# Attention kernel: the low rotary key products on 64 rows of TensorE, two score pieces at a time, with the rotary halves laid out by head

## The chip, the cores and the metric

The kernel runs on one core of one Trainium2 chip. The metric is the device time of one execution in microseconds; the median of three runs of the kernel before is 1512.42 us (1511.95 to 1512.44).

## What is computed

One layer over 2048 tokens of width 512: a layer norm, causal attention with a latent of 128 for keys and values and 16 heads, each head's key being 128 plain numbers and 64 rotary ones shared by all heads, and beside it a sum of eight 512x512 factors.

```python
q = (x @ wq).reshape(b, s, H, QH).transpose(0, 2, 1, 3)
q_nope, q_pe = (q[..., :NOPE], q[..., NOPE:])
kva = x @ wkv_a
ckv, k_pe = (kva[..., :LORA], kva[..., LORA:])
ckv = ckv * jax.lax.rsqrt(jnp.mean(ckv * ckv, axis=-1, keepdims=True) + EPS)
ckv = ckv * kv_norm_scale
kv = (ckv @ wkv_b).reshape(b, s, H, NOPE + VD).transpose(0, 2, 1, 3)
...
q_pe = _rope(q_pe, cos, sin)
k_pe = _rope(k_pe[:, None, :, :], cos, sin)
...
scores = jnp.einsum('bhqd,bhkd->bhqk', qs, ks_) * scale
...
attn = jax.nn.softmax(scores, axis=-1)
out = jnp.einsum('bhqk,bhkd->bhqd', attn, v)
```

## The kernel before

The weights of keys are absorbed into those of the queries, so that scores are products of a query's latent (128) and the common latent keys, plus a rotary part of 64. All operands are kept as two fp16 parts, a high one and a low one (the rest), and a product of two such numbers takes three products of TensorE: high with high, high with low, low with high.

Queries are taken in four chunks of 512, the last chunk first (`ORDER` is 3, 2, 1, 0). Within a chunk the 16 heads follow one another; a head of a chunk is a unit `i` (64 in all). A unit has four rows `r` of 128 queries, and a row of chunk `c` has `c + 1` score pieces `p` of up to 512 keys: 512 each and last `(r + 1) * 128`; for `r == 0` the last two are 384 and 256. So the first 16 units have four pieces in a row, the next 16 three, then two, then one.

A score piece is the function `scores`, with its products on lines 547, 548 and 549 (latent: `kTh` and `kTl` are the high and low keys, `q[:, i % 2, 0]` and `[1]` the high and low queries), 552 and 553 (rotary). The rotary query tile `q[:, i % 2, 2]` has 128 rows: the 64 high parts of the head and its 64 low parts. `kRh` and `kRl`, the rotary keys, stand twice in their 128 rows, so that L552 gives high and low queries with the high keys in one product, and L553 both with the low keys. Pieces go round four banks of PSUM (`s_bank`, `SBANKS = 4`): piece n waits for the exponentials of piece n - 4 (semaphore `a_exp`). L553 of a piece tells VectorE that it is done (`p_s`).

After the pieces of a row TensorE has other work in a fixed order written out by `fills(i, r)`: the next query products ("q", "pe"), value products of the unit before (`values`), output products (`head_output`), weights to be prepared in the first 16 units. `three` (lines 400 to 402) issues the three products of each of these.

Each row then goes: VectorE takes each piece's maximum (`maxima`: L1134 for whole pieces, L1136 with the causal mask for the last), the row's (L1146), and the bias `nm` (L1153); ScalarE takes the exponentials (`exps`, L781, with the sums) and their high parts (`high_parts`, L791); GpSimd takes the low parts (`low_parts`, L1354); SyncE's queue transposes both by DMA (L1539) for the value products of the next unit. On ScalarE, in rows 0 and 1 of the units with three or four pieces, the work that comes early (`early`: query read-out L764, output weights L748, rotary query L770) stands right behind the exponentials of piece 2 and the high part of piece 1, and ahead of the exponentials of piece 3 where there is one.

The rotary queries are made for two heads at once: `q_rope` on TensorE, then on VectorE L1121 to L1123 (cosine products of 128 rows, sine products of 2 times 64 rows, reading the other half), the sum on GpSimd (L1330), and for each head the copy of the high part on ScalarE (`rope_parts`, L770, all 128 rows of both heads) and on GpSimd two subtractions of 32 rows (L1345), which put the head's low parts over the other head's rows. The four blocks of 32 rows are ordered half first, head second. `load_wp` brings the rotary columns of the weights in four loads; `turned_keys` and `latent` make the rotary keys, in the opening.

Of the kernel before, what the change touches and what calls it, by code (L numbers as in the profile page):

```python
# [8 lines left out]
ALU = mybir.AluOpType  # L9
# [3 lines left out]
P = 128  # L13
# [3 lines left out]
CH = 512  # L17
# [33 lines left out]
def chunk(i):  # L51

    return ORDER[i // H]
# [12 lines left out]
def pieces(c, r):  # L66

    w = [CH] * c + [(r + 1) * P]
    if c and r == 0:
        w[c - 1:] = [CH - P, 2 * P]  # L70
    return [(sum(w[:p]), n) for p, n in enumerate(w)]
# [143 lines left out]
def build(nc, x, wq, wkv_a, wkv_b, wo, kvs, factors, bias, rope_t, rope_n, out):  # L215
    ctx = ExitStack()
    with ctx:
        def sb(name, shape, dt):
            return ctx.enter_context(nc.sbuf_tensor(name, shape, dt))
# [57 lines left out]
        rstd = sb("rstd", [P, 3, NT], F32)  # L277
        ssq = sb("ssq", [P, 3, NT], F32)
        ps = ctx.enter_context(nc.psum_tensor("ps", [P, 8, CH], F32))
        q = sb("q", [P, 2, 3, CH], F16)  # L280


        with ExitStack() as stage_one:
# [114 lines left out]
        def _(e):  # L398
# [132 lines left out]
            def scores(i, r, p):  # L531
                n = piece(i, r, p)
                k0, keys = pieces(chunk(i), r)[p]
                b = s_bank(n)[:, 0:keys]
                qs, ks = slice(r * P, (r + 1) * P), slice(k0, k0 + keys)
                if n >= SBANKS:
                    e.wait_ge(z["a_exp"], n - SBANKS + 1)
                if n < SBANKS:

                    e.wait_ge(z["v_kva"], NP - SBANKS + 1 + n)  # L540
                    e.wait_ge(z["a_kk"], NP - SBANKS + 1 + n)
                if i == 0 and r == 0 and p < NC - 1:

                    e.wait_ge(z["v_kT"], (p + 2) * QT // 2)
                if r == 0 and p == 0:
                    e.wait_ge(z["v_q"], i + 1)
                e.matmul(b, q[:, i % 2, 0, qs], kTh[:, ks], start=True, stop=False)  # L547
                e.matmul(b, q[:, i % 2, 0, qs], kTl[:, ks], start=False, stop=False)  # L548
                e.matmul(b, q[:, i % 2, 1, qs], kTh[:, ks], start=False, stop=False)  # L549
                if r == 0 and p == 0:  # L550
                    e.wait_ge(z["g_parts"], 2 * i + 2)
                e.matmul(b, q[:, i % 2, 2, qs], kRh[:, ks], start=False, stop=False)  # L552
                e.matmul(b, q[:, i % 2, 2, qs], kRl[:, ks], start=False, stop=True).then_inc(z["p_s"], 1)  # L553

            def values(i, part):

# [93 lines left out]
        def _(e):  # L650
# [53 lines left out]
            def squares(kind, i):  # L704

                w, at, total, load, loads = {
                    "sqp": (wsp[:, :, :].rearrange("p k n -> p (k n)"), 0, nrm[:, 2:3], "d_wp", 64),
                    "sq0": (wsq[:, 0, :, :].rearrange("p k n -> p (k n)"), E, nrm[:, 0:1], "d_wq0", 16),
                    "sq1": (wsq[:, 1, :, :].rearrange("p k n -> p (k n)"), 2 * E, nrm[:, 1:2], "d_wq1", 16),
                    "sqk": (wsk[:, i % 4:i % 4 + 2, :].rearrange("p a n -> p (a n)"), 3 * E, rows[:, 0:1], "g_sk", 1)}[kind]  # L710
                e.wait_ge(z[load], loads * (i // 2 + 1))
                if i:
                    e.wait_ge(z["p_nrm"], i // 2)
                    e.wait_ge(z["a_" + kind], i // 2)
                if i and kind == "sqk":
                    e.wait_ge(z["a_r4"], i // 2)
                square_sum(w, at, total).then_inc(z["a_" + kind], 1)
                if kind == "sqk":

                    e.wait_ge(z["a_sqk"], i // 2 + 1)  # L720
                    if i:
                        e.wait_ge(z["a_r8"], i // 2)
                    e.activation(rows[:, 1:2], rows[:, 0:1], ACT.Square).then_inc(z["a_r4"], 1)
                    e.wait_ge(z["a_r4"], i // 2 + 1)
                    e.activation(nrm[:, 3:4], rows[:, 1:2], ACT.Square).then_inc(z["a_r8"], 1)
# [40 lines left out]
            def rope_parts(i):  # L766
                e.wait_ge(z["g_rot"], i // 2 + 1)
                if i >= 2:
                    e.wait_ge(z["p_s"], FIRST[i - 1])
                e.activation(q[:, i % 2, 2, :], rot[:, 0, :], ACT.Copy).then_inc(z["a_parts"], 1)  # L770

            def exps(i, r, p):
# [124 lines left out]
        def _(e):  # L897
# [177 lines left out]
            def latent(p2):  # L1075
                b = latent_bank(p2)
                ts = slice(2 * p2, 2 * p2 + 2)
                rows = both(p2)
                cos = ropen[:, rows, 0, :].unsqueeze(2).broadcast_to([P, 2, 2, HALF])
                halves = b[:, :, LORA:QH].rearrange("p t (a n) -> p t a n", a=2)  # L1080
                turned = kt[p2 % 4][:, :, P:2 * P].rearrange("p t (a d n) -> p t a d n", a=2, d=2)
                if p2 == 0:
                    e.wait_ge(z["d_ropen"], 16)
                e.wait_ge(z["a_rms"], p2 + 1)
                e.reciprocal(ssq[:, 2, ts], ssq[:, 1, ts]).then_inc(z["v_rr"], 1)
                if p2 >= 4:
                    e.wait_ge(z["p_kT"], p2 - 3)
                e.tensor_tensor(turned[:, :, :, 0, :], halves, cos, ALU.mult)
                for a in range(2):

                    ins = e.tensor_tensor(ktmp[:, p2 % 4, :, a, :], halves[:, :, 1 - a, :], ropen[:, rows, 1 + a, :], ALU.mult)
                ins.then_inc(z["v_kva"], 1)
# [21 lines left out]
            def q_rope(i):  # L1114
                b = bank(("pe", i))
                if i % H == 0:
                    e.wait_ge(z["d_tab"], 16 * (i // H + 1))
                e.wait_ge(z["p_pe"], i // 2 + 1)
                if i:
                    e.wait_ge(z["g_parts"], 2 * i)  # L1120
                e.tensor_tensor(rot[:, 0, :], b, tab[:, 0, :], ALU.mult)  # L1121
                e.tensor_tensor(rot[0:ROPE, 1, :], b[ROPE:P, :], tab[0:ROPE, 1, :], ALU.mult)
                e.tensor_tensor(rot[ROPE:P, 1, :], b[0:ROPE, :], tab[ROPE:P, 1, :], ALU.mult).then_inc(z["v_pe"], 1)  # L1123

            def maxima(i, r, p):
                n = piece(i, r, p)
# [147 lines left out]
        def _(e):  # L1274
# [17 lines left out]

            def turned_keys(p2):

                turned = kt[p2 % 4][:, :, P:2 * P].rearrange("p t (a d n) -> p t a d n", a=2, d=2)
                e.wait_ge(z["v_kva"], p2 + 1)
                for d in (1, 0):
                    ins = e.tensor_tensor(turned[:, :, :, d, :], turned[:, :, :, 0, :], ktmp[:, p2 % 4, :, :, :],
                                          ALU.add)
                ins.then_inc(z["g_kk"], 1)  # L1300
# [31 lines left out]
            def rope_parts(i):  # L1332

                e.wait_ge(z["a_parts"], i + 1)
                if i == 0:
                    e.wait_ge(z["g_rot"], 1)
                    e.wait_ge(z["g_kk"], NP - 1)
                else:
                    r = 2 if i % H == 0 else 1 if i < (NC - 1) * H else 0
                    e.wait_ge(z["g_pL"], piece(i - 1, r, chunk(i - 1)) + 1)  # L1340
                hi = q[:, i % 2, 2, :]
                for half in range(2):
                    src = slice((2 * half + i % 2) * HALF, (2 * half + i % 2 + 1) * HALF)
                    dst = slice((2 * half + 1 - i % 2) * HALF, (2 * half + 2 - i % 2) * HALF)
                    e.tensor_tensor(hi[dst, :], rot[src, 0, :], hi[src, :], ALU.subtract).then_inc(  # L1345
                        z["g_parts"], 1)
                    e.wait_ge(z["g_parts"], 2 * i + half + 1)
# [59 lines left out]
        def _(e):  # L1407
# [39 lines left out]
            def load_wp(i):  # L1447
                if i:
                    e.wait_ge(z["v_wpe"], i // 2)

                for half in range(2):
                    for b in range(2):
                        at, src = (2 * half + b) * HALF, (i + b) * QH + NOPE + half * HALF
                        e.dma_start(wsp[:, :, at:at + HALF], wqv[:, :, src:src + HALF]).then_inc(z["d_wp"], 16)

            def load_factor(i):
                r, k4 = divmod(i, KE)
# [173 lines left out]
def rope_tables():  # L1631

    inv = (1.0 / np.float32(10000.0) ** (np.arange(0, ROPE, 2, dtype=np.float32) / np.float32(ROPE)))
    ang = (np.arange(S, dtype=np.float32)[:, None] * inv.astype(np.float32)).astype(np.float32)
    cos, sin = np.cos(ang), np.sin(ang)
    by_row = np.empty((P, 2, S), np.float32)
    cos, sin = cos * np.float32(BACK), sin * np.float32(BACK)
    by_row[:, 0] = np.tile(cos.T, (4, 1))
    by_row[:, 1] = np.concatenate([-sin.T, -sin.T, sin.T, sin.T])
    by_pos = np.stack([cos, -sin, sin], 1).reshape(NT, P, 3, HALF).transpose(1, 0, 2, 3)  # L1640
    return by_row, np.ascontiguousarray(by_pos)

# [18 lines left out]
```

## Time and profile before

| | |
|---|---|
| median of three runs | 1512.42 us |
| the profiled execution, its own time | 1514.25 us |
| its span, first to last instruction | 1512.4 us |
| TensorE (PE) busy | 1474.0 us, 97% |
| VectorE (DVE) busy | 1012.4 us, 67% |
| ScalarE (ACT) busy | 969.0 us, 64% |
| GpSimd (POOL) busy | 906.8 us, 60% |
| DMA queue q1, share of 16 engines' span | 73.6% |

Busy times overlap, so they don't add up. The four chunks can be told by the first products of L547 in units 0, 16 and 32, at 56.3, 604.4 and 1012.4 us; ahead of 56 us lies the opening, in which keys and values are made. Ends of TensorE's products in a trace are modelled, so its pace is read from starts.

### The profile page before, as it was taken

To read this page: it belongs to the slowest core of one execution; us is meant where nothing else is said; L and a number is where in the kernel's file an instruction comes from. 1 tells how busy PE (TensorE), PEld (TensorE's weight loads), DVE (VectorE), ACT (ScalarE), POOL (GpSimd) and SP (SyncE) were. 2 spreads that over 40 slices of the span, in tenths; PEclk is the share of its full clock that TensorE was granted. 3 is DMA by queue.
4 is the path that set the end of the run, shared out by engine and by line. 5 is a ranking of instruction groups with operands and counts; after the bars stand their busy time and mean duration, and the time that the engine had idled before them with its cause. 6 is when DMAs were issued, how large, how long until landed. Compare 5 with 4: busy or idle time off the path is not lost.

```text
span 1512.4 us, 25752 instructions
## 1 busy us (share of the span) xinstructions
PE 1474.0 (97%) x7908; PEld 757.4 (50%) x7908; DVE 1012.4 (67%) x2563; ACT 969.0 (64%) x2410; POOL 906.8 (60%) x913
## 2 busy tenths in 40 slices
PE   5899999999999999999999999999999999999997
PEld 5544555554454544545444444445555555455553
DVE  7767676777777766655556565566656666676776
ACT  7877777677766576666466666665556566554553
POOL 1688777766665465675465656656546555664552
PEclk9999999999999999999999999999999999999999
DMA  6499989897776598787577677877856777754554
GB/s 200 144 197 207 191 184 187 190 176 147 152 153 137 120 185 170 133 176 139 119 147 140 138 133 146 179 146 139 150 117 135 142 133 151 159 133 94 121 117 100
DMA packets 646615, 227.84 MB, mean 151 GB/s; under 512 B 599376, under 2 KB 612176, under 8 KB 646096
## 3 DMA queue, kind: packets, MB, share of 16 engines
q1 hardware_dynamic: 646480, 226.20, 73.6%
q8 instruction: 65, 1.06, 0.3%
q14 instruction: 70, 0.57, 0.1%
HBM read 65.67 MB, written 17.83 MB: 55 GB/s over the span
## 4 chain that ended last, share of the span: by engine, by line
PE 83%; DVE 6%; ACT 6%; issue 3%; DMA 1%; POOL 0%; ACTq 0%; SPq 0%; POOLq 0%; DVEq 0%
PE ps L400 17%; PE ps L401 17%; PE ps L402 16%; PE ps L547 7%; PE ps L552 6%; PE ps L553 6%; PE ps L549 6%; PE ps L548 6%; ACT ex L781 4%; DVE gm L1134 2%; DVE ps L1136 1%; DVE q L1111 0%; ACT wV L748 0%; DMA acc<-x_in 0%; DVE nm L1153 0%
## 5 line engine op out<-in xcount | busy, mean ns | idle before, releaser
L1354 POOL TENSOR_TENSOR st<-ex,st 128x512 f16<-128x512 f32 (+3 forms) x640 | 637.1, 1014 | 504.0 <-ACT st L791 493.8
L781 ACT ACTIVATE ex<-ps,nm,scales 128x512 f32<-128x512 f32 (+3 forms) x640 | 452.0, 709 | 466.8 <-DVE nm L1153 456.3
L1134 DVE TENSOR_REDUCE gm<-ps 128x1 f32<-128x512 f32 (+1 forms) x384 | 248.7, 668 | 168.6 <-PE ps L553 164.5
L791 ACT ACTIVATE st<-ex 128x512 f16<-128x512 f32 (+3 forms) x640 | 341.5, 562 | 5.9
L547 PE MATMUL ps<-kTh,q 128*128 128x512 f16 (+3 forms) x640 | 222.3, 347 | 8.0 <-ACT ex L781 5.7
L400 PE MATMUL ps<-pT,vH 128*128 128x512 f16 (+3 forms) x640 | 222.3, 347 | 2.3 <-DMA pT<-st 2.3
L552 PE MATMUL ps<-kRh,q 128*128 128x512 f16 (+3 forms) x640 | 222.2, 347 | 1.4 <-POOL q L1345 1.4
L401 PE MATMUL ps<-pT,vH 128*128 128x512 f16 (+3 forms) x640 | 222.4, 347 | 0.0
L549 PE MATMUL ps<-kTh,q 128*128 128x512 f16 (+3 forms) x640 | 222.2, 347 | 0.0
L553 PE MATMUL ps<-kRl,q 128*128 128x512 f16 (+3 forms) x640 | 222.2, 347 | 0.0
L548 PE MATMUL ps<-kTl,q 128*128 128x512 f16 (+3 forms) x640 | 222.2, 347 | 0.0
L402 PE MATMUL ps<-pT,vL 128*128 128x512 f16 (+3 forms) x640 | 219.2, 348 | 0.0
L1187 DVE SCALAR_TENSOR_TENSOR acc<-ps,rden,acc 128x512 f32<-128x512 f32 x256 | 189.7, 743 | 4.4 <-PE ps L402 4.0
L1345 POOL TENSOR_TENSOR q<-rot,q 32x512 f16<-32x512 f32 x128 | 148.8, 1162 | 25.6 <-ACT q L770 12.8
L1136 DVE CUSTOM_DVE_ANT_0 ps<-ps,cmask 128x256 f32<-128x256 f32 (+3 forms) x256 | 132.7, 518 | 25.6 <-PE ps L553 22.8
L781 ACT ACTIVATION_READ_ACCUMULATOR ex<-ps,nm,scales 128x1 f32 x640 | 125.7, 196 | 0.0
L1111 DVE SCALAR_TENSOR_TENSOR q<-ps,q 128x512 f16<-128x512 f32 x64 | 44.2, 690 | 112.5 <-ACT q L764 112.4
L400 PE MATMUL ps<-wV,oT 128*128 128x512 f16 x256 | 98.0, 383 | 4.7 <-issue 3.1
L547 PEld LDWEIGHTS ps<-kTh,q 128*128 128x128 f16 x640 | 62.5, 98 | 75.3 <-ACT ex L781 11.2
L401 PE MATMUL ps<-wV,oT 128*128 128x512 f16 x256 | 98.0, 383 | 0.0
L402 PE MATMUL ps<-wV,oT 128*128 128x512 f16 x256 | 97.8, 382 | 0.0
L400 PE MATMUL ps<-xT,wA 128*128 128x512 f16 x256 | 97.1, 379 | 0.0
(200 smaller groups left out, 2144.7 us busy)
## 6 DMA issues: line engine op xcount, KB each, us to landing
wA<-w_abs SPq DMA_DIRECT2D x48, 256.0 KB, 2.9
wV<-w_vo SPq DMA_DIRECT2D x48, 256.0 KB, 2.9
pT<-st SPq DMA_TRANSPOSE x640, 3.3
fland<-factors_in SPq DMA_DIRECT2D x28, 256.0 KB, 3.1
wP<-w_pe SPq DMA_DIRECT2D x24, 256.0 KB, 3.1
wsq<-wq_in SPq DMA_DIRECT2D x16, 256.0 KB, 3.8
wso<-wo_in SPq DMA_DIRECT2D x16, 256.0 KB, 3.1
w_abs<-wA SPq DMA_DIRECT2D x16, 256.0 KB, 2.3
```

The lines of the kernel that those rows point to most:

```text
L400: e.matmul(o, a[0], b[0], start=first, stop=False)
L401: e.matmul(o, a[0], b[1], start=False, stop=False)
L402: return e.matmul(o, a[1], b[0], start=False, stop=last)
L547: e.matmul(b, q[:, i % 2, 0, qs], kTh[:, ks], start=True, stop=False)
L548: e.matmul(b, q[:, i % 2, 0, qs], kTl[:, ks], start=False, stop=False)
L549: e.matmul(b, q[:, i % 2, 1, qs], kTh[:, ks], start=False, stop=False)
L552: e.matmul(b, q[:, i % 2, 2, qs], kRh[:, ks], start=False, stop=False)
L553: e.matmul(b, q[:, i % 2, 2, qs], kRl[:, ks], start=False, stop=True).then_inc(z["p_s"], 1)
L781: e.activation(ex[:, n % NEX, 0:keys], s_bank(n)[:, 0:keys], ACT.Exp, bias=nm[:, (i * QT + r) % 4:(i * QT + r) % 4 + 1], scale=scales[:, p ...
L791: e.activation(stage(n, keys)[:, :, 0, :], ex[:, n % NEX, 0:keys].rearrange("p (t n) -> p t n", n=P), ACT.Copy).then_inc(z["a_pH"], 1)
L1134: e.tensor_reduce(m, b, AX_X, ALU.max).then_inc(z["v_max"], 1)
L1354: e.tensor_tensor(s[:, :, 1, :], ex[:, n % NEX, 0:keys].rearrange("p (t n) -> p t n", n=P), s[:, :, 0, :], ALU.subtract).then_inc(z["g_pL" ...
```

## The change

1. `q` gets a fourth slot, `q[:, :, 3]`, which holds the 64 high rotary parts of the head twice, in rows 0 to 63 and 64 to 127. `rope_parts` on ScalarE writes it with two copies of 64 rows, ahead of the copy that was there.
2. L553 is replaced. For an odd piece p two products follow its L552: pieces p - 1 and p each with 64 rows (the low keys' first copy for the one, the second for the other), each telling of its own piece. The product of low queries and low keys, which was part of L553, is left out for them. The low product of an even piece is thereby issued behind the four first products of the piece after it. A last piece with an even number (chunks 2 and 0) keeps L553 with 128 rows.
3. The four blocks of 32 rows are ordered head first, half second, in the weights (`load_wp`: two loads of 64 columns for four of 32), the sine table, the keys (`turned`) and GpSimd's subtractions. VectorE's sine products become four of 32 rows.

```diff
@@ q
-        q = sb("q", [P, 2, 3, CH], F16)
+        q = sb("q", [P, 2, 4, CH], F16)
@@ scores
-                e.matmul(b, q[:, i % 2, 2, qs], kRl[:, ks], start=False, stop=True).then_inc(z["p_s"], 1)
+                if p % 2 == 0 and p == chunk(i):
+
+                    e.matmul(b, q[:, i % 2, 2, qs], kRl[:, ks], start=False, stop=True).then_inc(z["p_s"], 1)
+                elif p % 2:
+
+                    for half in range(2):
+                        k0, keys = pieces(chunk(i), r)[p - 1 + half]
+                        on, ks = slice(half * ROPE, (half + 1) * ROPE), slice(k0, k0 + keys)
+                        e.matmul(s_bank(n - 1 + half)[:, 0:keys], q[on, i % 2, 3, qs], kRl[on, ks], start=False,
+                                 stop=True).then_inc(z["p_s"], 1)
@@ squares (scalar)
-                    "sqp": (wsp[:, :, :].rearrange("p k n -> p (k n)"), 0, nrm[:, 2:3], "d_wp", 64),
+                    "sqp": (wsp[:, :, :].rearrange("p k n -> p (k n)"), 0, nrm[:, 2:3], "d_wp", 32),
@@ rope_parts (scalar)
+
+                mine = slice(i % 2 * ROPE, (i % 2 + 1) * ROPE)
+                for half in range(2):
+                    e.activation(q[half * ROPE:(half + 1) * ROPE, i % 2, 3, :], rot[mine, 0, :], ACT.Copy)
                 e.activation(q[:, i % 2, 2, :], rot[:, 0, :], ACT.Copy).then_inc(z["a_parts"], 1)
@@ latent (vector) and turned_keys (gpsimd)
-                turned = kt[p2 % 4][:, :, P:2 * P].rearrange("p t (a d n) -> p t a d n", a=2, d=2)
+                turned = kt[p2 % 4][:, :, P:2 * P].rearrange("p t (d a n) -> p t a d n", a=2, d=2)
@@ q_rope (vector)
-                e.tensor_tensor(rot[0:ROPE, 1, :], b[ROPE:P, :], tab[0:ROPE, 1, :], ALU.mult)
-                e.tensor_tensor(rot[ROPE:P, 1, :], b[0:ROPE, :], tab[ROPE:P, 1, :], ALU.mult).then_inc(z["v_pe"], 1)
+                for n in range(4):
+
+                    to, of = slice(n * HALF, (n + 1) * HALF), slice((n ^ 1) * HALF, ((n ^ 1) + 1) * HALF)
+                    ins = e.tensor_tensor(rot[to, 1, :], b[of, :], tab[to, 1, :], ALU.mult)
+                ins.then_inc(z["v_pe"], 1)
@@ rope_parts (gpsimd)
-                    src = slice((2 * half + i % 2) * HALF, (2 * half + i % 2 + 1) * HALF)
-                    dst = slice((2 * half + 1 - i % 2) * HALF, (2 * half + 2 - i % 2) * HALF)
+                    src = slice((2 * (i % 2) + half) * HALF, (2 * (i % 2) + half + 1) * HALF)
+                    dst = slice((2 - 2 * (i % 2) + half) * HALF, (3 - 2 * (i % 2) + half) * HALF)
@@ load_wp (sync)
-                for half in range(2):
-                    for b in range(2):
-                        at, src = (2 * half + b) * HALF, (i + b) * QH + NOPE + half * HALF
-                        e.dma_start(wsp[:, :, at:at + HALF], wqv[:, :, src:src + HALF]).then_inc(z["d_wp"], 16)
+                for b in range(2):
+                    src = (i + b) * QH + NOPE
+                    e.dma_start(wsp[:, :, b * ROPE:(b + 1) * ROPE], wqv[:, :, src:src + ROPE]).then_inc(z["d_wp"], 16)
@@ rope_tables
-    by_row[:, 1] = np.concatenate([-sin.T, -sin.T, sin.T, sin.T])
+    by_row[:, 1] = np.concatenate([-sin.T, sin.T, -sin.T, sin.T])
```

## Rows read from the trace of the kernel before

**Rows 1.** The page: busy us of the engines, and the chain that ended last.

```profile
PE 1474.0 (97%) x7908; PEld 757.4 (50%) x7908; DVE 1012.4 (67%) x2563; ACT 969.0 (64%) x2410; POOL 906.8 (60%) x913
...
PE 83%; DVE 6%; ACT 6%; issue 3%; DMA 1%; POOL 0%; ACTq 0%; SPq 0%; POOLq 0%; DVEq 0%
```

**Rows 2.** TensorE in order of time, unit 8, row 0: start us, us, what.

```profile
323.81 0.38 PE L547 MATMUL ps<-kTh,q 128*128 128x512 f16 x1
...
325.97 0.33 PE L547 MATMUL ps<-kTh,q 128*128 128x384 f16 x1
...
326.78 0.27 PE L547 MATMUL ps<-kTh,q 128*128 128x256 f16 x1
...
327.22 0.27 PE L553 MATMUL ps<-kRl,q 128*128 128x256 f16 x1
```

**Rows 3.** Stretches: length, busy us of each engine, granted clock, DMA share, GB/s.

```profile
56.50:609.00 552.50, 542.92 (x2895) 275.33 (x2894) 397.55 (x1000) 393.54 (x991) 371.49 (x359) 1.00 0.83 167
609.00:1000.00 391.00, 391.00 (x1995) 193.22 (x1994) 230.99 (x545) 244.68 (x597) 234.22 (x226) 1.00 0.75 146
...
1300.00:1512.00 212.00, 200.86 (x1115) 103.67 (x1113) 151.92 (x395) 108.25 (x259) 108.14 (x114) 0.98 0.53 115
```

**Rows 4.** TensorE's groups by shape: busy us, mean ns, idle before.

```profile
L553 PE MATMUL ps<-kRl,q 128*128 128x512 f16 x400 | 151.6, 379 | 0.0
...
L553 PE MATMUL ps<-kRl,q 128*128 128x384 f16 x112 | 36.5, 326 | 0.0
...
L553 PE MATMUL ps<-kRl,q 128*128 128x256 f16 x112 | 30.5, 273 | 0.0
```

**Rows 5.** In order of time, unit 8: fp32 transposes between fp16 products.

```profile
335.36 0.60 PE L424 MATMUL ps<-ident,wsq 128*128 128x128 f32 x4
...
335.79 0.27 PE L431 MATMUL ps<-ident,wsk 128*128 128x128 f32 x1
...
336.01 0.38 PE L400 MATMUL ps<-pT,vH 128*128 128x512 f16 x1
```

**Rows 6.** Weight loads in order of time, behind a wait, unit 8.

```profile
342.91 0.10 PEld L547 LDWEIGHTS ps<-kTh,q 128*128 128x128 f16 x1 [0.76 <-ACT ex L781]
```

**Rows 7.** In order of time, unit 7, rows 1 and 2: ScalarE and TensorE.

```profile
308.36 0.62 ACT L770 ACTIVATE q<-rot 128x512 f16<-128x512 f32 x1
...
308.88 0.56 ACT L781 ACTIVATE ex<-ps,nm,scales 128x256 f32<-128x256 f32 x1
...
309.32 0.20 ACT L781 ACTIVATION_READ_ACCUMULATOR ex<-ps,nm,scales 128x1 f32 x1
...
309.91 0.33 PE L547 MATMUL ps<-kTh,q 128*128 128x384 f16 x1
```

**Rows 8.** VectorE in order of time, unit 8, row 0.

```profile
326.17 1.37 DVE L1134 TENSOR_REDUCE gm<-ps 128x1 f32<-128x512 f32 x2 [0.39 <-PE ps L553]
327.53 0.43 DVE L1136 CUSTOM_DVE_ANT_0 ps<-ps,cmask 128x256 f32<-128x256 f32 x1
327.88 0.14 DVE L1136 DVE_READ_ACCUMULATOR2_ANT gm<- 128x1 f32 x1
```

**Rows 9.** In order of time, unit 8, rows 1 and 2.

```profile
342.66 0.20 ACT L781 ACTIVATION_READ_ACCUMULATOR ex<-ps,nm,scales 128x1 f32 x1
...
342.92 0.34 PE L547 MATMUL ps<-kTh,q 128*128 128x384 f16 x1 [0.26 <-ACT ex L781]
```

**Rows 10.** TensorE's waits, 56 to 609 us: us in total, times, longest.

```profile
PE ps L547 <- ACT ex L781: 5.7, 10, 1.4
```

**Rows 11.** ScalarE in order of time, at the turn to unit 8.

```profile
325.72 0.20 ACT L781 ACTIVATION_READ_ACCUMULATOR ex<-ps,nm,scales 128x1 f32 x1
```

**Rows 12.** The chain that ended last, opening: start us, us, what.

```profile
44.07 0.69 DVE rot L1121
...
45.48 0.68 DVE rot L1123
...
47.00 0.33 PE ps L493
```

More of the change, by code:

```diff
@@ L1293, in turned_keys @@
             def turned_keys(p2):
-                turned = kt[p2 % 4][:, :, P:2 * P].rearrange("p t (a d n) -> p t a d n", a=2, d=2)
+                turned = kt[p2 % 4][:, :, P:2 * P].rearrange("p t (d a n) -> p t a d n", a=2, d=2)
                 e.wait_ge(z["v_kva"], p2 + 1)
```

## The prediction

> **What bounds the kernel now.** I read the page's busy shares and its chain of waits first: TensorE is busy 1474.0 us of 1512.4 and holds 83% of the chain that ended last [rows 1]. A busy TensorE need not be a full one, so I read the pace next, in the list of instructions in order of time. Ten score products of 512 columns start between 323.81 and 325.97 us, 0.216 us each; five of 384 columns take 0.81 us (0.162 each) and four of 256 take 0.44 (0.11 each) [rows 2]. That is a stream without holes at 2.4 GHz, so a column saved is time saved wherever TensorE does not then wait. The table of stretches shows where it does not wait today: from 609 to 1000 us (three pieces) it is busy 391.00 of 391.00 us, in the first chunk (56.5 to 609 us) 542.92 of 552.50, at the granted clock of 1.00 [rows 3]. The other engines are busy 60 to 67% on average, but each row of scores has a loop through them: last score of a row, its maximum on VectorE, the bias, four exponentials on ScalarE, and only then a free bank for the next row's last piece. How much play that loop has decides the change.
>
> **The products that go.** The fifth product of a score piece (L553) streams 512, 384 or 256 columns or 128 [rows 4]. A pair (pieces 0 and 1, and 2 and 3) now runs its two fifth products on different halves of the rows; if they run together, a pair costs the longer one. Columns saved by a unit (one head of one chunk) are the shorter of each pair, over its four rows: with four pieces 512+256, 512+256, 512+384 and 512+512, so 3456; with three 384+512+512+512 = 1920; with two 256+256+384+512 = 1408; with one none. Times 16 heads and 0.216 us for 512: 23.3 + 13.0 + 9.5 = 45.8 us, in 128 + 64 + 64 = 256 pairs. This saving has two preconditions that no row of before shows, since all products there use 128 rows: that the halves run side by side, and that going from 128 rows to 64 and back is cheap.
>
> **What a pair costs besides.** From below: nothing, and not less, since no work disappears other than the columns counted. From above: TensorE lets the last product leave the array before each of the two changes of form. A 512-column product has a record of 379 ns at a pace of 216, so 0.163 us lie behind the stream (its end is modelled), 0.33 us a pair [rows 2, 4]. The nearest rows on changing the way of working are the fp32 transposes between fp16 products: 335.36 to 335.79, then 336.01, each at its stream's time, no gap [rows 5]. An exposed weight load is seen after a wait: load at 342.91, product at 342.92 [rows 6]. I take 0.015 us a pair, nearest to these rows: 240 pairs, 3.6 us (of 256, some 16 lie ahead of a wait that swallows it). The Trainium skill, "TensorEngine Tiling (Array Packing)", Key Properties, says that changing the tiling mode, other than the tile, drains TensorE; the first rival below is what that would do here. Its page "TensorE: Matmul & The Clock Gate", Part 3, says of row tiles that products on distinct row groups start some 4 ns apart, which would give the 45.8 us; no run shows either yet.
>
> **What ScalarE and VectorE get, and what is late next.** Two copies of 64 rows go ahead of the copy at L770, in row 1 of a unit, before its last exponential. A copy takes ScalarE 0.52 us (308.36 to 308.88) [rows 7]; half the rows hold as many elements each, so I price two at 1.04 us. Queued behind them are the exponential of piece 3, the high parts and through them GpSimd; waiting for that exponential is TensorE's piece 3 of row 2. Count the play of this boundary in the first chunk, where four pieces use all four banks. (a) TensorE comes sooner after its own last score of row 1: pair 0/1 is 0.216 us shorter and piece 2's low product moves behind piece 3, another 0.216: 0.43. (b) Piece 2 and 3 are released together, so piece 2's maximum (half of 1.37 us, 0.68) no longer lies under piece 3's products (0.54 us for 256 columns); VectorE already runs close behind, 326.17 to 327.53 for the 512s and on to 327.88 [rows 8]. That is 0.54 us later, 0.68 for wider last pieces. (c) 1.04 us of copies. Together 2.0 us. The play today: in unit 7 the reading of the exponential's sum ends at 309.52 and TensorE starts at 309.91, 0.39 us [rows 7]; a stall of 1.6 us is due. In unit 8 TensorE waits already, 0.26 us, until the same reading ends at 342.86 and its product starts at 342.92 [rows 9]; there VectorE's scale work is what is late, (b) is only the 0.33 us by which TensorE's row ends sooner, and the stall grows by 1.8. Today such waits make 5.7 us in ten [rows 10], which stay. I take 7 and 8 for odd and even units and 13 of 16 units, since unit 0 and two late ones have more play or take the copies elsewhere: 13 x 1.75 = 22.8 us. At the turn from row 3 to the next unit's row 0 the play is 326.78 - 325.92 = 0.86 us [rows 2, 11] against 0.38 (piece 2 has 384 columns) + 0.68: 0.2 us in 14 units, 2.8. The turns from row 0 and row 2 I leave at nothing: their play hides it, and without that cover each would cost up to 0.5 us a unit, 8 us. So the first chunk gives back 25.6 us and earns nothing of its 23.3.
> With three pieces or two, a row does not use all four banks and the copies come behind the last exponential; I cost them at nothing, covered by TensorE's fills, and the 22.5 us stay. With one piece nothing is gained and ScalarE gets 1.04 us a unit in a stretch where TensorE is busy 200.86 of 212 [rows 3]: 0 to 3 us, taken as 0.
>
> **Small edits.** The rotary sums take four operations of 32 rows where two of 64 stood; each is as long as its 512 columns, 0.69 us, so 1.38 us a pair of heads on VectorE, and GpSimd's sum behind it. In the loop they stand where VectorE waits for scores anyway. In the opening they don't: rot starts at 44.07, the third ends at 46.16, the key parts follow, and a transpose of TensorE waits for these until 47.00 [rows 12]. That is 1.4 us on the path. The opening's copies end before the query product does. The two loads of 64 rotary columns for four of 32 take two issues off SyncE's queue for each pair of heads and move the same bytes, nothing gained as nobody on the path waits for them; the orders of halves in keys, queries and sine table change places, not counts; GpSimd's two operations per head stay.
>
> **The sum.** -45.8 + 25.6 + 3.6 + 1.4 = -15.2 us on the profiled execution's 1514.25, which stands 1.8 above the median of 1512.42: 1499.1 there, 1497 as a median.
>
> **Rivals.** 1. Slower: TensorE empties at every change of form. For it: the 0.163 us behind each stream must go somewhere if the array may not hold both forms. Against it: [rows 5]. It decides from (45.8 - 25.6 - 1.4)/240 = 0.078 us a pair. With those terms alone the sum is -18.8. At half the bound, 0.163 a pair, 39.1 us come on top: +20.3, 1533; at the full bound 78.2 us, +59.4, 1572. 2. The change doesn't do what it says: the halves run one after the other. Then no column is saved, the deferral (0.216), the later maximum (some 0.4 odd, 0 even) and the copies still cost row 2 some 1.28 us in 13 units, 16.6, and the opening 1.4: 1530. 3. The loop has more play than I count, and 15 of the 25.6 us of stalls don't come: 1482. 4. A change of form costs about 0.08 us a pair: all is eaten, 1512.
>
> **How the numbers follow.** Forecast 0.42 (its own range 1487 to 1508), rival 1 0.27, rival 2 0.15, rival 3 0.08, rival 4 0.08. Some 0.2% (3 us) is about what a measurement of this kernel can tell from no change. Faster: forecast and rival 3 less an edge, 0.48. Same: rival 4 and the edge, 0.09. Slower: 0.43. The range reaches from rival 3 to a drain of three quarters of its bound (58.7 - 18.8 = 39.9), 1482 to 1552; outside lie some 0.05 below and 0.12 above.
>
> **What would show it.** Side by side: L553's successors of a pair start within 0.05 us of each other; serial: 0.2 us apart. Drain: gaps of 0.04 us and more ahead of the 64-row products and behind them, in the stretch behind 609 us too. Stalls: TensorE waiting for the exponential some 25 us more, nearly all before 609 us, ahead of piece 3 of row 2; the first chunk as long as before and the stretches with three and two pieces 13.0 and 9.5 us shorter. I am wrong if the first chunk shrinks by over 10 us, if copies of 64 rows take other than 0.5 us, or if the opening does not grow by a microsecond.

## The result and the profile after

The changed kernel takes 1559.62 us (median of four runs, 1555.75 to 1562.61) against 1512.29 us for the kernel before: 1.0312 of its time, 95% interval 1.0285 to 1.0339, 47 us slower. The forecast was 1497 us, and the time lies above its range of 1482 to 1552.

The page of the changed kernel, the lines that answer to [rows 1], and two groups of its fifth part (busy us, mean ns, idle time before them and what ended it):

```profile
PE 1491.4 (96%) x7908; PEld 710.2 (46%) x7908; DVE 1045.7 (67%) x2627; ACT 1049.6 (67%) x2538; POOL 906.7 (58%) x913
...
PE 75%; ACT 9%; DVE 9%; issue 4%; DMA 1%; POOL 0%; ACTq 0%; SPq 0%; POOLq 0%; DVEq 0%
...
L547 PE MATMUL ps<-kTh,q 128*128 128x512 f16 (+3 forms) x640 | 224.1, 350 | 30.0 <-ACT ex L794 27.5
...
L561 PE MATMUL ps<-kRl,q 64*128 64x512 f16 (+2 forms) x512 | 98.4, 367 | 0.0
```

TensorE's share of the chain fell from 83% to 75%, and ScalarE and VectorE have 9% each instead of 6. The low products (L561, and L555 for the pieces without a partner, 39.2 us) are busy 137.6 us together where L553 was busy 222.2, so columns did go. But the chain has waits that were not there, and TensorE's records, which overlap, hide something else, which only the list in order of time shows. From 609 us on, in the stretch of three pieces:

```profile
700.79 0.38 PE L552 MATMUL ps<-kRh,q 128*128 128x512 f16 x1
701.11 0.39 PE L561 MATMUL ps<-kRl,q 64*128 64x512 f16 x2
701.43 0.28 PE L547 MATMUL ps<-kTh,q 128*128 128x256 f16 x1
```

and the weight loads in the same place:

```profile
701.10 0.10 PEld L561 LDWEIGHTS ps<-kRl,q 64*128 64x128 f16 x2 [0.42 <-issue]
...
701.42 0.10 PEld L547 LDWEIGHTS ps<-kTh,q 128*128 128x128 f16 x1 [0.23 <-issue]
```

Two products stand in one row of 0.39 us, as long as one: they run side by side, the second starting 3 or 4 ns behind the first in 254 of the 256 pairs. The Trainium skill, "TensorE: Matmul & The Clock Gate", Part 3, says about 4 ns for row tiles, and the trace agrees. But L552 starts at 700.79 and at a pace of 0.216 us the pair was due at 701.01; it starts at 701.11. It streams to 701.33, and the next product starts at 701.43. Both times TensorE stands still for 0.10 us. The weight load, which elsewhere is issued under the running product, comes only at the end of the gap, 0.01 us ahead of its product, as close as behind a plain wait [rows 6]. So load and product are held back together, and the gap is not the time of the load.

Where the time went, by stretch: the opening, and then the chunks with four, three, two and one pieces in a row, told by the first product of L547 in units 0, 16, 32 and 48 of each trace (us; the next section describes the kernels of the other rows):

| kernel | opening | four | three | two | one |
|---|---|---|---|---|---|
| before | 56.3 | 548.1 | 408.0 | 297.1 | 202.9 |
| changed | 58.4 | 581.7 | 409.8 | 302.9 | 207.1 |
| e1_layout | 57.8 | 550.2 | 408.1 | 299.6 | 207.7 |
| e10_four_ops | 57.3 | 548.5 | 408.1 | 299.6 | 207.9 |
| e2_copies | 58.9 | 564.1 | 408.1 | 299.6 | 208.8 |
| e3_defer | 57.6 | 554.2 | 409.2 | 299.6 | 209.0 |
| e4_pairs128 | 57.4 | 576.1 | 409.2 | 300.4 | 208.3 |
| e5_same_rows | 58.5 | 592.1 | 421.6 | 311.6 | 206.4 |
| e6_single64 | 57.5 | 596.2 | 448.2 | 323.4 | 217.6 |
| e7_copies_late | 58.3 | 553.3 | 409.8 | 302.9 | 207.2 |
| e11_pairs128_late | 58.3 | 552.2 | 409.2 | 299.7 | 210.0 |
| e9_batch | 58.5 | 614.6 | 410.5 | 303.6 | 207.0 |
| e9b_batch_late | 58.8 | 577.9 | 410.5 | 303.4 | 206.9 |
| e8_before_late | 56.1 | 545.0 | 408.0 | 297.1 | 203.0 |

No stretch got shorter. The four pieces have 33.6 of the 47.5 us.

In these 33.6 us lies a term that no list of waits shows. TensorE's granted clock fell to half four times among the four pieces of the changed kernel, for 17.1 us in all, 16.3 of them busy; in the kernel before it was once, for 3.4 us. Two of the four (columns as in [rows 3]):

```profile
89.20:92.61 3.41, 3.41 (x10) 1.22 (x8) 0.99 (x2) 3.16 (x10) 2.84 (x4) 0.50 1.03 195
...
147.23:154.06 6.83, 6.09 (x16) 2.04 (x17) 3.76 (x8) 4.51 (x12) 5.25 (x5) 0.50 0.51 101
```

At half the clock half of the busy time is lost: an estimate of 8.2 us against 1.7, 6.5 us more. How often the clock falls differs from trace to trace (not at all in this stretch of e10_four_ops, 10.2 us in e4_pairs128), so differences of a few us in the column of four pieces need a look at it.

### The profile page after: what moved, and what is told of

The parts are those of the page before. It is cut to its first block, busy times and chain, and to the rows that moved or that the text cites. A ratio compares the mean times of both kernels' runs of the same rounds, so it can differ in the third digit from the quotient of the medians.

```text
span 1560.0 us, 25928 instructions
## 1 busy us (share of the span) xinstructions
PE 1491.4 (96%) x7908; PEld 710.2 (46%) x7908; DVE 1045.7 (67%) x2627; ACT 1049.6 (67%) x2538; POOL 906.7 (58%) x913
## 4 chain that ended last, share of the span: by engine, by line
PE 75%; ACT 9%; DVE 9%; issue 4%; DMA 1%; POOL 0%; ACTq 0%; SPq 0%; POOLq 0%; DVEq 0%
PE ps L400 16%; PE ps L402 15%; PE ps L401 15%; PE ps L547 7%; PE ps L552 6%; PE ps L549 6%; PE ps L548 6%; ACT ex L794 5%; PE ps L561 4%; DVE gm L1150 2%; PE ps L555 1%; ACT q L782 1%; DVE ps L1152 1%; ACT wV L757 1%; DVE rot L1138 1%
## 5 line engine op out<-in xcount | busy, mean ns | idle before, releaser
L1150 DVE TENSOR_REDUCE gm<-ps 128x1 f32<-128x512 f32 (+1 forms) x384 | 244.8, 668 | 215.3 <-PE ps L561 214.4
L547 PE MATMUL ps<-kTh,q 128*128 128x512 f16 (+3 forms) x640 | 224.1, 350 | 30.0 <-ACT ex L794 27.5
L552 PE MATMUL ps<-kRh,q 128*128 128x512 f16 (+3 forms) x640 | 222.6, 348 | 3.0 <-POOL q L1361 3.0
L547 PEld LDWEIGHTS ps<-kTh,q 128*128 128x128 f16 x640 | 62.2, 97 | 116.5 <-ACT ex L794 43.2
L561 PE MATMUL ps<-kRl,q 64*128 64x512 f16 (+2 forms) x512 | 98.4, 367 | 0.0
```

The costliest lines, as they stand in the source:

```text
L1150: e.tensor_reduce(m, b, AX_X, ALU.max).then_inc(z["v_max"], 1)
```

## The experiments

Two theories stood against each other. One: the change of rows (from products of 128 rows to products of 64 and back) eats what the columns give. The other: the loop of maxima, exponentials and banks carries the loss. The first kernels put the parts of the change in one by one.

**The layout alone.** The low product is as before, the copies are out; what is left is the order of halves and VectorE's four operations.

```diff
@@ scores
...
-                elif p % 2:
...
-                    for half in range(2):
...
+                e.matmul(b, q[:, i % 2, 2, qs], kRl[:, ks], start=False, stop=True).then_inc(z["p_s"], 1)
@@ rope_parts (scalar)
-                mine = slice(i % 2 * ROPE, (i % 2 + 1) * ROPE)
-                for half in range(2):
-                    e.activation(q[half * ROPE:(half + 1) * ROPE, i % 2, 3, :], rot[mine, 0, :], ACT.Copy)
```

> The changed kernel with the low product of each piece put back as it was (128 rows, right behind the piece's other four) and without the two copies of 64 rows: the change of layout alone, with VectorE's four sine products of 32 rows. Both theories, that of the change of rows (TensorE pays some 0.1 us at each change between 128 and 64 rows) and that of the loop (waits for the exponentials carry the loss), put the layout at little: 1514 to 1519 us, about 2 us of it in the opening, nothing in the stretches of three and two pieces.

Measured: 1524.85 us, 1.0076 of before (1.0061 to 1.0091). Both theories were too low here; the table puts 4.8 us into the stretch of one piece and 2.5 into that of two. In the stretch of one piece, VectorE and TensorE in order of time in the layout kernel:

```profile
1389.18 2.79 DVE L1126 TENSOR_TENSOR rot<-ps,tab 32x512 f32<-32x512 f32 x4
...
1392.64 0.68 DVE L1176 SCALAR_TENSOR_TENSOR oT<-ps,oT 128x512 f16<-128x512 f32 x1
...
1393.42 0.38 PE L400 MATMUL ps<-wV,oT 128*128 128x512 f16 x1 [0.48 <-issue]
```

and VectorE at the same point of a later pair of heads in the kernel before, with TensorE's product:

```profile
1466.04 0.68 DVE L1123 TENSOR_TENSOR rot<-ps,tab 64x512 f32<-64x512 f32 x1
...
1467.39 0.68 DVE L1172 SCALAR_TENSOR_TENSOR oT<-ps,oT 128x512 f16<-128x512 f32 x1
...
1468.93 0.38 PE L400 MATMUL ps<-wV,oT 128*128 128x512 f16 x1
```

The rotary operations are followed on VectorE by the row's maximum, the bias and the low part of the values' output (`oT`), for which TensorE's output product waits. Before, that part ended at 1468.07, 0.86 us ahead of the product. VectorE's 1.38 us more are 0.5 too many, and TensorE stands 0.64 us behind its pace in five of the stretch's eight pairs of heads and 1.20 in a sixth, 4.4 us (in the stretch of two pieces 0.42 in six of eight, 2.5 us). The trace names "issue" as what ended the wait, since the releasing engine had just been done.

**VectorE's operations alone, in the kernel before.**

```diff
-                e.tensor_tensor(rot[0:ROPE, 1, :], b[ROPE:P, :], tab[0:ROPE, 1, :], ALU.mult)
-                e.tensor_tensor(rot[ROPE:P, 1, :], b[0:ROPE, :], tab[ROPE:P, 1, :], ALU.mult).then_inc(z["v_pe"], 1)
+                for n in range(4):
+                    to, of = slice(n * HALF, (n + 1) * HALF), slice((n ^ 2) * HALF, ((n ^ 2) + 1) * HALF)
+                    ins = e.tensor_tensor(rot[to, 1, :], b[of, :], tab[to, 1, :], ALU.mult)
+                ins.then_inc(z["v_pe"], 1)
```

> The kernel before with VectorE's two sine products of 64 rows split into four of 32, the order of halves as it was. Doubles the one suspected cost of the layout. If the 12.7 us of the layout kernel are VectorE's 1.4 us more for each pair of heads, ahead of the read-out of the values' output and TensorE's output product: 1521 to 1527. If they are of the order of halves in memory (loads, keys): 1512 to 1515.

Measured: 1524.61 us, 1.0078 (1.0061 to 1.0095), as expected the same as the layout kernel, and the same by stretches but for the four pieces, where the layout kernel has 1.7 us more and also 3.4 us at half clock, which this trace has not. The layout's cost is the count of operations; the order of halves costs nothing that these runs can tell.

**The copies, and the order of the low products.** The second kernel adds the two copies to the layout kernel, whose low products don't read them; the third leaves them out and issues the low products of two pieces together with 128 rows; the fourth has both.

```diff
@@ e3_defer and e4_pairs128, against the changed kernel
-                        on, ks = slice(half * ROPE, (half + 1) * ROPE), slice(k0, k0 + keys)
-                        e.matmul(s_bank(n - 1 + half)[:, 0:keys], q[on, i % 2, 3, qs], kRl[on, ks], start=False,
+                        ks = slice(k0, k0 + keys)
+                        e.matmul(s_bank(n - 1 + half)[:, 0:keys], q[:, i % 2, 2, qs], kRl[:, ks], start=False,
```

> The layout and the two copies on ScalarE, whose result no product reads; the low products as before. With 1.04 us more ahead of the last exponential of row 1, the play of 0.39 us of the odd units and of nothing in the even ones gives 0.65 and 1.04 us in 13 units of the first chunk, 11 us: 1525 to 1530. The theory of the loop as the whole cause wants more, 1540 and up.

> The layout, and the low products of two pieces issued together behind the second piece's four, but each with all 128 rows (no copies): the later release of the even piece alone. Play 0.39 against 0.65 us in odd units and 0.2 us in even ones: 3 us, 1516 to 1522. If the later maxima were what carries the loss: 1535 and up.

> All of the change but the 64 rows: layout, copies, the order of the low products, each with 128 rows. Theory of the change of rows: the stall of row 2 costs some 1.3 us in 13 units, the small edits 6: 1532 to 1542, and 15 to 25 us less than the changed kernel, though 45.8 us more columns are streamed; the stretches of three and two pieces are as long as before (408.0 and 297.1 us). Theory of the loop: 1555 and up, no less than the changed kernel.

Measured: 1542.14 us (1.0187, 1.0169 to 1.0205), 1533.21 (1.0139, 1.0122 to 1.0156) and 1553.67 (1.0269, 1.0254 to 1.0284). Against the layout kernel's 1524.85 the copies cost 17 us, the order of products 8, and both together 29. Each part alone cost more than expected (1525 to 1530 for the copies, 1516 to 1522 for the order); the copies' time is one that the theory of the loop had asked for (1540 and up). 14 of the copies' 17 us lie in the four pieces, where TensorE waits for exponentials (kernel with the copies, 58 to 630 us; us in total, times, longest):

```profile
PE ps L547 <- ACT ex L785: 21.7, 17, 2.3
```

against 5.7 us in ten waits before [rows 10] and 7.0 in twelve in the layout kernel. With 128 rows and all the rest of the change the kernel is only 6 us faster than with the 64-row pairs. That was above what the theory of the change of rows expected (1532 to 1542) and near what the theory of the loop did (1555 and up): for this kernel the loop and the layout carry 41 of the 47 us. It doesn't say that the change of rows is cheap, as the 45.8 us of columns are gone too; the next two kernels price that.

**Both halves on the same rows.**

```diff
-                        on, ks = slice(half * ROPE, (half + 1) * ROPE), slice(k0, k0 + keys)
+                        on, ks = slice(0, ROPE), slice(k0, k0 + keys)
```

> The changed kernel with both products of a pair on rows 0 to 63, instead of on different halves. If the halves now run side by side, this takes it away and nothing else: the 45.8 us of columns come back, 1600 to 1610 us (some of it hidden under the first chunk's waits: not under 1585). If they ran one after the other already, no difference: 1555 to 1565.

Measured: 1592.85 us, 33 us more than the changed kernel: more than nothing, and less than the 40 to 50 expected, with 11.8 us in the three pieces and 8.7 in the two, where the columns saved are worth 13.0 and 9.5, and 10.4 of 23.3 in the four pieces. In order of time:

```profile
700.88 0.38 PE L552 MATMUL ps<-kRh,q 128*128 128x512 f16 x1
701.19 0.60 PE L561 MATMUL ps<-kRl,q 64*128 64x512 f16 x2
701.73 0.39 PE L547 MATMUL ps<-kTh,q 128*128 128x512 f16 x1
```

The pair now takes 0.54 us from start to next start, where it took 0.32; the gaps of 0.10 before and behind are the same. So the halves do run side by side in the changed kernel, and the columns are saved as computed, to within 2 us of 22.5 where TensorE hardly waits. In the four pieces part of the saving was time that TensorE then spent waiting: its waits for exponentials fall from 27.1 to 18.3 us, and its time at half clock from 17.1 to 10.2.

**A 64-row product alone in every piece.** Against the layout kernel (no copies, no pairs; the product of low queries and low keys is left out):

```diff
-                e.matmul(b, q[:, i % 2, 2, qs], kRl[:, ks], start=False, stop=True).then_inc(z["p_s"], 1)
+                on = slice(i % 2 * ROPE, (i % 2 + 1) * ROPE)
+                e.matmul(b, q[on, i % 2, 2, qs], kRl[on, ks], start=False, stop=True).then_inc(z["p_s"], 1)
```

> The layout kernel (e1_layout) with each piece's low product on 64 rows, alone and right behind the piece's other products; no copies, no pairs, as many columns as before. The product of low queries and low keys is left out. Each of 640 products brings a change to 64 rows and one back. At 0.1 us each, 128 us more than the layout kernel's 1524.9, some of it under waits of the first chunk: 1635 to 1655. If the change of rows is free and the gaps seen in the changed kernel came from something else in a pair: 1520 to 1530.

Measured: 1645.23 us, 120.4 more than the layout kernel for 640 products: 0.19 us each. In the stretch of three pieces, where nothing hides it, 448.2 - 408.1 = 40.1 us for 192 products, 0.209 each. In order of time:

```profile
700.49 0.38 PE L552 MATMUL ps<-kRh,q 128*128 128x512 f16 x1
700.80 0.39 PE L554 MATMUL ps<-kRl,q 64*128 64x512 f16 x1
701.12 0.34 PE L547 MATMUL ps<-kTh,q 128*128 128x384 f16 x1
```

The same 0.10 us on both sides, without a pair and without copies. Nor is it the change of banks that comes with the order of a pair: the kernel with pairs of 128 rows has that order too, and its stretch of three pieces is 409.2 us. That is the change of rows, and it is shown. A pair of the changed kernel pays 0.2 us, 256 of them 51 us, for 45.8 us of columns. The Trainium skill, "TensorEngine Tiling (Array Packing)", Key Properties, says that changing the tiling mode drains TensorE; the traces agree that something of that kind takes 0.10 us at every change.

**The copies out of the way.** The changed kernel, and the one with pairs of 128 rows, with the first chunk's rotary copies (the two new ones and the one that was there) behind the row's high parts.

```diff
-                    early = ("q", "wo", "parts", "sqv") + (("sq1",) if i == 0 else ())
+                    early = ("q", "wo", "sqv") + (("parts",) if last < 3 else ()) + (("sq1",) if i == 0 else ())
```

> The changed kernel with the rotary copies of the first chunk's units moved behind the high parts of their row, on ScalarE, so that the last exponential of row 1 does not wait for them. If it is these copies that make TensorE wait ahead of piece 3 of row 2: the first chunk loses 13 to 20 us of its 581.7, 1540 to 1547 in all. If the wait is set by the maxima: under 5 us gained, 1555 and up.

> As e7_copies_late, but with all 128 rows in every low product: the pair of 64-row products against two of 128 rows with the waits of the first chunk out of the way. 256 pairs give 45.8 us of columns and cost 256 x 0.2 = 51 us of changes, so this should be some 5 us faster than e7_copies_late: 1528 to 1533. If the side by side pairs were a gain on their own, this would be slower, 1545 and up.

Measured: 1535.61 us (1.0148, 1.0133 to 1.0163) and 1527.89 (1.01, 1.0085 to 1.0115). The first is 24 us faster than the changed kernel, more than the 13 to 20 expected. In the traces it is 28.4 us, all in the four pieces (581.7 to 553.3): 20.2 of waits for exponentials, and the 8.2 of the clock, which did not fall there at all. TensorE's waits for exponentials in its whole trace (6.9 of the 7.3 us in the four pieces), and in the changed kernel from 58 to 640 us:

```profile
PE ps L547 <- ACT ex L794: 7.3, 13, 1.8
```

```profile
PE ps L547 <- ACT ex L794: 27.1, 19, 2.5
```

The place of the copies is the cause of most of the waits ahead of piece 3 of row 2 (22.6 us in 14 of the 16 units, 2.4 us in seven with the copies moved): shown by moving them alone. The second kernel is 7.7 us faster than the first, though it streams 45.8 us more: with most of the waits out of the way the pair of 64-row products is a loss. 256 x 0.2 - 45.8 = 5.4 us was due, and the runs of either kernel spread over 3 to 4 us.

**Fewer changes of rows.** The low products of a whole row of four pieces in one batch, with the copies early and late.

```diff
-                elif p % 2:
+                elif p == chunk(i) and p % 2:
 
-                    for half in range(2):
-                        k0, keys = pieces(chunk(i), r)[p - 1 + half]
+                    for m in range(p + 1):
+                        k0, keys = pieces(chunk(i), r)[m]
...
```

> The changed kernel with the four low products of a row of the first chunk (and the two of the third) issued together behind the row's last piece: half the changes of rows in the first chunk. At 0.2 us a change and back, 64 fewer give 12.8 us; within the batch no gap is due between the first pair and the second, if it is the change that costs and not the 64-row product. Against it, three pieces' maxima now come behind the row (1.4 us later than in the changed kernel), which the turns of all four rows have to bear: 1580 to 1610. If only the number of changes counted: 1547.

> The same batch of four with the rotary copies moved behind the row as in e7_copies_late (1535.6). If the maxima decide: 1555 to 1590. If the number of changes decides: 1523.

Measured: 1594.32 and 1557.84 us, 35 and 22 us slower than with two batches a row. The batch itself is what it should be:

```profile
299.75 0.27 PE L552 MATMUL ps<-kRh,q 128*128 128x256 f16 x1
299.95 0.60 PE L561 MATMUL ps<-kRl,q 64*128 64x512 f16 x4
300.49 0.39 PE L400 MATMUL ps<-wV,oT 128*128 128x512 f16 x1
```

Four products take 0.54 us to the next start: two times 0.216 and one gap of 0.10, none between the pairs. But all four maxima now come behind the row, and TensorE waits for exponentials 46.0 us in 34 waits. Its clock fell more often too, to 34.1 us at half among the four pieces. Both times lie in the expected ranges. What a batch saves in changes it gives back in the loop. No version with another count of banks was run, so whether a loop with more play could keep the gain stays open.

**The kernel before with the copy moved.** The same edit of `early` in the kernel before, nothing else.

> The kernel before with one thing moved: in the first chunk's units the rotary copy on ScalarE comes behind the high parts of its row, not ahead of the last exponential. The play at piece 3 of row 2 grows by 0.52 us, so most of TensorE's 5.7 us of waits for exponentials go: 1507 to 1511. If what is late next is GpSimd's low parts or the last maximum: 1512.

Measured: 1510.66 us (11 runs, 1508.48 to 1511.47), 0.9981 of before (0.9972 to 0.9989), as expected: the fastest of all kernels here, by some 2 us. The 3.1 us come out of the four pieces (548.1 to 545.0), where the wait shrank:

```profile
PE ps L547 <- ACT ex L781: 3.0, 3, 1.4
```

## Why the prediction was wrong

What bounds the kernel, and the columns. Right: a column saved is time saved where TensorE doesn't wait, and rival 2, that the halves run one after the other, is excluded by the same-rows kernel. 45.8 us were computed, and the same-rows kernel gave back 20.5 of 22.5 in the stretches of three and two pieces.

What a pair costs besides. Wrong, and this step decides. I bounded it between nothing and 0.33 us a pair and took 0.015, "nearest to these rows". The rows were fp32 transposes between fp16 products, which change the type and not the number of rows, and an exposed weight load. Neither was near the thing in question. Measured: 0.20 us a pair, 51 us where 3.6 stood, 47 of the 62 us by which the forecast missed. The Trainium skill, "TensorEngine Tiling (Array Packing)", Key Properties, names exactly this change as one that drains TensorE, and I gave it 0.27. Rival 1 was this mechanism, at 0.163 a pair against 0.20 measured; its turning point, 0.078, was computed and passed by a factor of 2.6. It gave 1533 at that price, and at 0.20 it would have given 1542 (-18.8 + 48), still short of 1559.6, for what follows.

ScalarE's copies and VectorE's maxima. The mechanism was right: the place (piece 3 of row 2), the boundary and the kind of stall. Waits for exponentials in the first chunk grew from 5.7 to 27.1 us, 21.4, where 25.6 were forecast. In units 3 and 4:

```profile
187.17 0.34 PE L547 MATMUL ps<-kTh,q 128*128 128x384 f16 x1 [0.96 <-ACT ex L794]
...
222.34 0.50 PE L547 MATMUL ps<-kTh,q 128*128 128x384 f16 x1 [2.18 <-ACT ex L794]
```

An even unit's wait grew by 1.9 us (1.8 forecast); an odd unit's is 1.0 (1.6 forecast), so there was more play in the odd units than I had read from unit 7. Ahead of piece 3 of row 2 the waits grew by 19.6 us in all where 22.8 stood (13 x 1.75; the mean of my own 1.6 and 1.8 is 1.7), and the turn to the next unit, priced at 2.8, got none. A size was off the other way, the copies' price. In unit 2 of the changed kernel, and in unit 7 of the kernel before:

```profile
144.63 0.81 ACT L757 ACTIVATE wV<-wso,eps,vsc 128x512 f16<-128x512 f32 x1
145.46 1.26 ACT L782 ACTIVATE q<-rot 64x512 f16<-64x512 f32 x2
146.74 0.63 ACT L783 ACTIVATE q<-rot 128x512 f16<-128x512 f32 x1
147.27 0.55 ACT L794 ACTIVATE ex<-ps,nm,scales 128x256 f32<-128x256 f32 x1
```

```profile
307.65 0.81 ACT L748 ACTIVATE wV<-wso,eps,vsc 128x512 f16<-128x512 f32 x1
308.36 0.62 ACT L770 ACTIVATE q<-rot 128x512 f16<-128x512 f32 x1
```

The two copies take 1.28 us and not 1.04, and the first of them starts 0.83 us behind the operation ahead of it, where L770 started 0.71 behind: some 1.4 us in all. The book of that chunk reads: -23.3 of columns, +25.6 of changes (128 pairs), +21.4 of waits for exponentials, 23.7 in all, and 33.6 were measured. Of the 10 us left 6.5 are TensorE's clock (above), a term that the prediction didn't have, and 1.0 is in its waits for VectorE; 2.4 are not settled.

Small edits. Wrong by a wait that I didn't look up. "In the loop they stand where VectorE waits for scores anyway" holds nearly for the first chunk (0.4 us there with the operations alone; 2.1 in the layout kernel, whose clock fell there as often as before), not for who waits behind it in the chunks of two pieces and one: 2.5 and 5.0 us in e10_four_ops. The opening was right: 1.4 forecast, 2.1 in the changed kernel and 1.0 with the operations alone.

The range. It ended at three quarters of a full drain with all else as forecast. The time lay 8 us above, since the price of a change and the small edits were off the same way.

## What to carry to other kernels

Before products of fewer rows are run side by side, count the changes of form and not the columns alone: here each cost 0.10 us, so a pair of 512-column products just paid for its change and back (0.216 against 0.20), and shorter ones lost. A row of a trace bounds the cost of another operation only if it shares the thing in question. And when work is added to an engine with idle time, look at who waits for the operations queued behind it, unit by unit in each kind of unit: moving the rotary copies behind the last exponential took 24 us off the changed kernel, while the columns saved, less their changes, gave nothing.

## What the runs showed of the hardware

- Going from 128-row products to 64-row ones, and back, stops TensorE for 0.10 us each time (start to next start less the product's columns at 0.216 us for 512: 0.096 and 0.103 in the mean of e6_single64's 640 products), whatever the width of the products before and behind (128 to 512 columns); between 64-row pairs of one batch there is no gap.
- On ScalarE a copy of 64 rows x 512 has a record of 0.63 us like one of 128 rows, but the next operation started 0.64 us later instead of 0.52 to 0.54 (145.46 to 146.74 for two, 146.74 to 147.27 for one of 128 rows). What follows differs too, a copy there and an exponential here; no run separates the two.
- At long waits, or within 1.3 us behind them, TensorE's granted clock fell to half in the stretch of four pieces of the changed kernel (waits of 2.55, 2.54, 2.18 and 2.18 us), but not each time: the waits of 2.18 us that ended at 295.38 and 366.86 have no fall behind them. Around the wait of 2.54 us in unit 2 the stretches of the changed kernel show a mean of 0.66 where it was 1.00 just before, and the products of 384 columns behind it start 0.32 us apart, the 1.2 GHz level, instead of 0.162:

```profile
144.00:154.00 10.00, 7.46 (x23) 2.44 (x23) 6.06 (x12) 7.63 (x18) 7.03 (x7) 0.66 0.64 143
130.00:144.00 14.00, 14.00 (x73) 6.58 (x73) 10.96 (x41) 10.00 (x27) 8.96 (x9) 1.00 1.06 195
```

```profile
147.97 0.50 PE L547 MATMUL ps<-kTh,q 128*128 128x384 f16 x1 [2.54 <-ACT ex L794]
148.26 0.53 PE L548 MATMUL ps<-kTl,q 128*128 128x384 f16 x1
148.58 0.53 PE L549 MATMUL ps<-kTh,q 128*128 128x384 f16 x1
```
